# Gated feed-forward products over pairs of token tiles, a turned block of four heads' shifts, and window values laid out by tokens, in a fused sparse-attention and expert kernel

## What is computed

```
q, k, v   = 16 heads of width 16 from xn @ Wq, xn @ Wk, xn @ Wv
out_c     = softmax(q . compressed k of 32 blocks of 16 tokens) @ compressed v
top       = the 4 best blocks of each query
out_s     = softmax over the tokens of those 4 blocks @ v
out_l     = softmax over the last 33 tokens (a window) @ v
attention = (g0 out_c + g1 out_s + g2 out_l) @ Wo,   g = softmax(mean q @ Wg + bg)
mlp       = silu(xn @ Wg + bg) * (xn @ Wu + bu) @ Wd + bd,   1024 inner rows
experts   = product-key lookup: 4 heads, 8 of 1024 experts each, silu of their down product
out       = x + attention + mlp + experts
```

## Time and profile before

| | before |
|---|---|
| median of 3 runs | 1509.58 us (1504.55 to 1510.39) |
| the profiled execution's own time | 1507.87 us |
| its span | 1506.1 us |
| granted TensorE clock, mean | 0.979 of full |
| busy: PE, DVE, ACT, POOL | 1420.1, 1187.8, 928.4, 919.1 us |

### The profile page before, as it was taken

The page is one execution under the profiler, slowest core; times in us unless marked ns, Lnnn a source line. Parts: engine busy times, 40 slices in busy tenths (PEclk is TensorE's granted clock), DMA queues, the critical chain, the costliest instruction groups (busy, mean ns, idle before and its releaser), DMA issues. The chain is left out here.

```text
span 1506.1 us, 43877 instructions
## 1 busy us (share of the span) xinstructions
PE 1420.1 (94%) x14960; PEld 1044.1 (69%) x14960; DVE 1187.8 (79%) x4544; ACT 928.4 (62%) x1684; POOL 919.1 (61%) x845
## 2 busy tenths in 40 slices
PE   6899679999999999999999999999999999999978
PEld 4566447777777777777777777777777777777657
DVE  5444288888888888888888888898888888888812
ACT  3766336666666666666666666666666666666641
POOL 4655356666666666666666666666666666666620
PEclk8999879999999999999999999999999999999989
DMA  6556942221111122222111122212222222222027
GB/s 186 205 183 211 274 73 53 52 51 45 47 45 47 50 51 51 51 51 50 47 46 46 47 50 49 48 48 51 51 51 51 51 51 51 65 51 53 9 95 234
DMA packets 217147, 113.74 MB, mean 76 GB/s; under 512 B 128872, under 2 KB 211224, under 8 KB 217112
## 3 DMA queue, kind: packets, MB, share of 16 engines
q1 hardware_dynamic: 216304, 112.88, 27.3%
q10 hardware_dynamic: 808, 0.42, 0.2%
HBM read 73.08 MB, written 40.16 MB: 75 GB/s over the span
## 5 line engine op out<-in xcount | busy, mean ns | idle before, releaser
L1150 POOL TENSOR_TENSOR sumxy<-xy 128x1024 f32<-128x1024 f32 x128 | 240.7, 1901 | 0.0
L1393 DVE TENSOR_REDUCE bmax<-q_bank 128x32 f32<-128x512 f32 (+3 forms) x512 | 219.9, 481 | 16.5 <-PE q_bank L1633 15.4
L1240 ACT ACTIVATE pts<-k_bank 128x512 f32<-128x512 f32 (+2 forms) x384 | 177.4, 490 | 42.0 <-PE k_bank L1668 41.2
L1494 DVE SCALAR_TENSOR_TENSOR mw<-sumxy,c,ex 128x1024 f32<-128x1024 f32 x128 | 176.0, 1394 | 1.5 <-issue 0.8
L1633 PE MATMUL q_bank<-ko,qo 96*128 96x512 bf16 (+3 forms) x512 | 142.9, 306 | 24.6 <-DVE bmax L1393 22.6
L1116 POOL TENSOR_TENSOR pad<-pad 128x1 f32<-128x1 f32 x32 | 6.2, 193 | 256.4 <-DVE top L1412 256.4
L1615 PE MATMUL f_bank<-xt,wfu 128*128 128x128 f32 x1024 | 162.3, 281 | 0.0
L1174 POOL TENSOR_TENSOR cw<-cw,mw 128x1024 f32<-128x1024 f32 x64 | 150.8, 2356 | 6.6 <-ACT mw L1264 1.6
L1615 PE MATMUL f_bank<-xt,wfg 128*128 128x128 f32 x1024 | 150.3, 279 | 0.0
L1615 PEld LDWEIGHTS f_bank<-xt,wfu 128*128 128x128 f32 x1024 | 139.4, 191 | 11.5
L1264 ACT ACTIVATE mw<-mw,erec 128x1024 f32<-128x1024 f32 x128 | 145.7, 1139 | 0.0
(11 more groups left out here) (211 smaller groups left out, 3340.1 us busy)
## 6 DMA issues: line engine op xcount, KB each, us to landing
qo<-s_qs SPq DMA_DIRECT2D x192, 64.0 KB, 2.2
ko<-s_ks SPq DMA_DIRECT2D x186, 64.0 KB, 2.2
s_qs<-parts SPq DMA_DIRECT2D x8, 768.0 KB, 4.7
s_ks<-parts SPq DMA_DIRECT2D x8, 768.0 KB, 6.3
s_v<-vo SPq DMA_DIRECT2D x8, 544.0 KB, 3.0
vv<-s_v SPq DMA_DIRECT2D x32, 136.0 KB, 2.3
vw<-s_v SPq DMA_DIRECT2D x64, 68.0 KB, 2.5
xin<-in_L_attn_x_dram SPq DMA_DIRECT2D x8, 512.0 KB, 6.9
```

The lines of the kernel that those rows point to most:

```text
L1150: done("sum_done", g_.tensor_tensor(sumxy[:, h, :, :], xy[:, 0, h, 0:XK, None].broadcast_to([P, XK, KEYS]), xy[:, 1, h, None, :].broadcast ...
L1240: last = s.activation(pts[:, h, OFFS[j]:OFFS[j] + n], bank[:, 0:n], ACT.Exp)
L1393: last = v.tensor_reduce(bmax[:, i, h, 0:n], Q.bank(job)[:, o:o + n * BLK].rearrange("p (n j) -> p n j", j=BLK), AX.X, ALU.max)
L1494: done("mw_done", v.scalar_tensor_tensor(mw[:, h, :], sumxy[:, h, :, :].rearrange("p a b -> p (a b)"), c8[:, h, 7:8], ex[:, h % 2, :], ALU ...
```

## The change

1. **MLP up by pairs.** A unit moves both token tiles of its pair (`xp`, 256 tokens), but does half of the inner rows (4 `t.half` on). `up_rows` does one product of 256 columns in each call instead of two of 128. `mlp_down` adds 4 blocks of inner rows for each of the two tiles into Y, which now holds both tiles and is read once a pair; `xb` and `yo` follow.
2. **Shifts turned at once.** One `head_shifts` with 128 standing columns (4 heads by 32) fills one bank `a`. Head h's shift then stands in partitions 32h to 32h + 31, so `qo` and `ko` hold head h's shift or one-hot rows there and its q or k parts in the other three quarters; the places of shift rows are filled with zeros by DMA until the shift is there, and `queries` and `window` use 128 rows. ACT copies the four parts one by one: head 0 in `openings`, head 1 after `share(t, 2)`, heads 2 and 3 between the exponentials of head 0. Only the copy for head 3 releases the bank.
3. **Window values by tokens.** `local_values` has `pT` (32 columns) standing and `vw` (17 columns) moving and writes tokens by partitions, in two halves with the last `mlp_down` part split around the first; ACT's copy and PE's transposes of it go.
4. **Small ones.** DVE's `expert_sum` moves ahead of `key_marks`; some semaphores are merged.

The lists and loads (cut):

```
-            k_jobs = ["pcT", "co", "a0"]
+            k_jobs = ["pcT", "co", "a"]
             for h in range(HG):
-                k_jobs += [f"s{h}0", f"s{h}1", f"s{h}2"] + [f"a{h + 1}"] * (h < HG - 1) + [("pl0", "pl1", "vl", "tl")[h]]
-            k_jobs += ["vs", "ts"]
+                k_jobs += [f"s{h}0", f"s{h}1", f"s{h}2"] + [f"pl{h}"] * (h < 2)
+            k_jobs += ["vl", "vs", "ts"]
+            PARTS = ((0, 0), (2, 0)), ((0, 1), (0, 2)), ((1, 0), (1, 1))
+            N_NEAR, N_KEYS, N_QUERIES, N_LATE = (3, 4), 16, 20, (7, 8)
+            def part_rows(to, src, which, half):
+                for i, pair in enumerate(PARTS):
+                    lots = [(3, i, i + 1)] + [(i, h0, h1) for h0, h1 in ((0, i), (i + 1, HG)) if h0 < h1]
+                    for quad, h0, h1 in lots:
+                        for n in range(2):
+                            o = 32 * quad + D * n
+                            yield to[o:o + D, half, h0:h1, :], src[pair[n][which]][:, h0:h1, :]
                 def load_parts(b, g, half, keys=True):
+                    pairs = [(qo[32 * h:32 * h + 32, half, h, :], s_zero) for h in range(HG)]
+                    pairs += part_rows(qo, q, 0, half)
+                    if keys:
+                        pairs += part_rows(ko, k, 1, half)
```

ACT:

```
                         K.released(f"s{h}{j}", last)
-                    if h < HG - 1:
-                        head_shifts(t, h + 1)
+                        if h == 0 and j < 2:
+                            head_shifts(t, j + 2)
...
-                    if job == "g0":
-                        Y.wait_free(act, t, "y")
...
                 def head_shifts(t, h):
-                    K.wait_full(act, t, f"a{h}")
-                    K.released(f"a{h}", s.activation(qo[SP3:P, t.half, h, :], K.bank(f"a{h}")[SP3:P, :], ACT.Copy))
+                    if h == 0:
+                        K.wait_full(act, t, "a")
+                    rows = slice(32 * h, 32 * h + 32)
+                    copy = s.activation(qo[rows, t.half, h, :], K.bank("a")[rows, :], ACT.Copy)
+                    if h < HG - 1:
+                        done("aug_done", copy)
+                    else:
+                        K.released("a", copy)
...
                     share(t, 2)
+                    head_shifts(t, 1)
                     head(t, 0)
```

PE:

```
-                    o = P * (4 * j + k)
-                    dst = F.bank(f"{name}{j}")[:, k * P:k * P + P]
-                    for c in range(2):
-                        last = mm(dst, w_[:, c, o:o + P], xt[:, t.half, c, :], start=False, stop=(c == 1),
-                                  skip_group_check=True)
+                    f, c = divmod(k, 2)
+                    o = P * (4 * t.half + 2 * j + f)
+                    last = mm(F.bank(f"{name}{j}")[:, 2 * P * f:2 * P * f + 2 * P], w_[:, c, o:o + P], xp[:, c, :],
+                              start=False, stop=(c == 1), skip_group_check=True)
...
                 def keys_rows(t, h, part):
-                    if part == 0:
-                        K.wait_read(pe, t, f"a{h}")
+                    if part == 0 and h < HG - 1:
+                        need(pe, "aug_done", t, h + 1)
+                    elif part == 0:
+                        K.wait_read(pe, t, "a")
                     job = f"s{h}{part}"
                     K.wait_free(pe, t, job)
...
+                def local_values(t, r):
                     bank = K.bank("vl")
+                    rows = slice(64 * r, 64 * r + 64)
+                    for k in range(2):
+                        for g in range(T // 32):
+                            i, q = divmod(g, 4)
+                            o = VW * (HG * i + 2 * r + k)
+                            last = mm(bank[32 * q:32 * q + 32, o:o + VW], pT[rows, k, 32 * g:32 * g + 32],
+                                      vw[rows, t.half, g, VW * k:VW * k + VW], start=True, stop=True, skip_group_check=True)
...
                     for i in range(TT):
-                        last = mm(K.bank(f"a{h}")[SP3:P, P * i:P * i + P], shift_s[:, i, h, :], identb[:, :],
-                                  start=True, stop=True)
-                    K.filled(f"a{h}", last)
+                        last = mm(K.bank("a")[:, P * i:P * i + P], shift_s[:, i, :, :].rearrange("p h n -> p (h n)"),
+                                  identb[:, :], start=True, stop=True)
+                    K.filled("a", last)
...
-                            elif h == 2:
-                                local_ready(t)
-                            else:
-                                token_values(t, 1)
                             if h < 3:
                                 up_rows(t, "ugu"[h], (0, 1, 1)[h], part)
-                            else:
+                            elif part < 3:
                                 mlp_down(t, part)
-                            if (h, part) == (2, 3):
-                                local_values(t)
+                            if (h, part) == (3, 2):
+                                local_ready(t)
                             if n and part < 3:
                                 queries(n, h, part)
-                            if part == 2 and h < HG - 1:
-                                head_shifts(t, h + 1)
+                    local_values(t, 0)
+                    mlp_down(t, 3)
+                    local_values(t, 1)
                     selected_values(t)
```

More of the change, by code:

```diff
@@ L74, in count, with round @@
         return self.pair * (2 * per) + (self.offset * per + n)
+    def round(self):
+        return Round(self.pair, 0)
     def next(self, ahead=1):
         return Turn(self.pair, self.offset + ahead, step=self)
+class Round(Turn):
+    def count(self, per, n):
+        return self.pair * per + n
 class Chain:
@@ L1001, in hidden @@
             def hidden(j):
-                return hT[:, 4 * j:4 * j + 4, :].rearrange("p f t -> p (f t)")
+                return hT[:, 2 * j:2 * j + 2, :].rearrange("p f t -> p (f t)")
             def loaded_by(eng, lot, n, t):
+                n = n if isinstance(n, int) else n[t.half]
                 eng.wait_ge(lot[t.half], t.pair * (16 * n) + 16 * n * (t.offset // 2 + 1))
@@ L1039, in load_late @@
                           (gt[:, half, :, :].rearrange("p i n -> p (i n)"), row(s_gt, b)),
-                          (xb[:, half, :], row(tiles, b)[g]),
-                          *windows(b, g, half)], late_in[half], N_LATE)
+                          *both, *windows(b, g, half)], late_in[half], N_LATE[half])
                 def windows(b, g, half):
@@ L1183, in result_in @@
                     loaded_by(pool, late_in, N_LATE, t)
-                    done("xb_done", g_.tensor_tensor(xb[:, t.half, :], xb[:, t.half, :], bdb[:, :], ALU.add))
+                    done("xb_done", g_.tensor_tensor(xb[:, :, :], xb[:, :, :], bdb[:, None, :].broadcast_to([P, 2, C]), ALU.add))
                 def branches(t):
@@ L1312, in openings, with selected_values @@
                     tanh(t, "g0", hidden(0), "th_done")
-                def branch_values(t, k):
-                    job = ("vs", "vl")[k]
-                    K.wait_full(act, t, job)
-                    K.released(job, s.activation(oT[:, k, :], K.bank(job)[:, :], ACT.Copy))
+                def selected_values(t):
+                    K.wait_full(act, t, "vs")
+                    K.released("vs", s.activation(oT[:, :], K.bank("vs")[:, :], ACT.Copy))
                 def lead(n):
@@ L1593, in step @@
                     normalize(t, 0)
-                    result(t)
+                    if t.half:
+                        result(t)
                     cf.end()
@@ L1632, in queries @@
                         n = P * (i + 1)
-                        last = mm(bank[:, o:o + n], qo[0:SP3, t.half, h, P * i:P * i + P], ko[0:SP3, t.half, h, 0:n],
+                        last = mm(bank[:, o:o + n], qo[:, t.half, h, P * i:P * i + P], ko[:, t.half, h, 0:n],
                                   start=True, stop=(i > 0))
@@ L1693, in local_ready @@
                         K.wait_read(pe, t, f"pl{k}")
-                def local_values(t):
+                def local_values(t, r):
                     bank = K.bank("vl")
-                    for g in range(T // 32):
-                        for h in range(HG):
-                            rows, k = slice(64 * (h // 2), 64 * (h // 2) + 64), h % 2
-                            last = mm(bank[32 * h:32 * h + VW, 32 * g:32 * g + 32], vw[rows, t.half, g, VW * k:VW * k + VW],
-                                      pT[rows, k, 32 * g:32 * g + 32], start=True, stop=True, skip_group_check=True)
-                    K.filled("vl", last)
+                    rows = slice(64 * r, 64 * r + 64)
[5 more added lines that the diff above has]
+                                      vw[rows, t.half, g, VW * k:VW * k + VW], start=True, stop=True, skip_group_check=True)
+                    if r == 0:
+                        done("vl_half", last)
+                    else:
```

(6 more changed lines are left out.)

165 lines of the change are left out of this document (88 added, 77 removed).

## The result

The changed kernel takes 1597.01 us (median of 4, 1595.94 to 1602.08) against 1509.57 before: a ratio of 1.059, 95% interval 1.056 to 1.063. It is slower, as forecast, but by 87 us where I had 46, and 2 us above my range.

A forecast was written before the change was run, and what follows sets the result against it. PE bounds the step, except DVE from p01 to p21; +2.0 - 0.33 - 0.44 - 0.15 + 0.2 + 0.1 = +1.4 us a step, with the start 46 us on 1507.9: 1554 us, range 1503 to 1595.

The forecast's parts named there:

- The mechanism: PE waits ahead of s02 for ACT's last copy of bank a, 2.3 us; DVE then loses 2.0 us at p01.
- bank a holds nothing up: Rival at s02: PE is not held up and the savings win, 38.1 us a step, 1482 us; chance 0.14.
- both cancel: Rival: stall of 1.5 us against savings at their upper bounds, +0.4 us at most, 1508 to 1520 us; chance 0.12.
- The rival of cheap wide moving sides: Up products: half the weight loads take half the time, -1.1 us in place of -0.15, 1525 us; chance 0.08.
- The rival of SP's queue: Loads: at 0.5 to 0.6 us an issue, parts come 1.4 to 5 us late, 1600 to 1700 us; chance 0.08.
- the copy chain: ACT's copies with exponentials between, 2.57 us, ending at 734.71, so s02 starts 2.3 us late; +2.0 us a step.
- My upper bound: Stall of s02: 2.5 us if each of ACT's copies takes its full 0.59 us.
- the segment behind p21: Stretch at PE's pace, where savings count in full: head shifts -0.33 us, window value transposes -0.44 us.
- DVE's 2.25 us for candidates: DVE's wait for POOL's candidates would vanish with the earlier sum, worth nothing as PE sets the pace there.
- the window products: The 64 window value products, 1.39 us, stay and move behind s32 with sides exchanged; change taken as 0.
- the start: Start of the stage: 20 DMAs a queue ahead of the first queries instead of 6, 2 us, at most 6.4.
- the loads: 36 DMAs a unit instead of 12 on SP, landing 19.2 us after s32, cover nearly used up; +0.2 us a step.

The follow-up runs named there:

- experiment 1: Changed kernel with all four of ACT's shift copies ahead of the tanh of g0: 1532.42 us, ratio 1.015.
- experiment 2: Changed kernel with ACT's copies for heads 0 and 1 before the tanh of g0, 2 and 3 behind it, share 2 after the s00 exponential: 1504.13 us, ratio 0.996.
- experiment 9: Changed kernel with share 2 on ACT moved behind the exponentials of s01 and the last copy: 1551.11 us, ratio 1.028.
- experiment 11: Kernel before with only the shifts turned at once, including its 36 loads and zeros: 1616.93 us, ratio 1.072.
- experiment 5: Kernel before with only the paired up products, paired down product and paired result: 1506.45 us, ratio 0.998.
- experiment 3: Changed kernel with DVE's sum over the shares back behind the block maxima of head 2: 1611.63 us, ratio 1.067.
- experiment 6: Kernel before with paired products and window values by tokens and late, DVE's sum at its old place: 1521.44 us, ratio 1.009.
- experiment 7: Changed kernel with ACT's copies spread around the tanh and DVE's second up product ahead of unselected marks and best pairs: 1484.76 us, ratio 0.984.
- experiment 4: Kernel before with its 12 part loads split into 36 DMAs a unit and the setup store of zeros: 1528.97 us, ratio 1.012.

## Why the prediction was right and wrong

**The mechanism held.** PE idles ahead of s02 in each step, ended by ACT's last copy; experiments 1, 2, 9 and 11 take this wait away, shorten it or make it alone, and the time follows. DVE waits 2.59 us for p01 behind it. Rivals one and two (bank a holds nothing up; both cancel) fell with it. The rival of cheap wide moving sides fell as well: experiment 5 gains 0.2%. The rows have 0.22 to 0.24 us for an f32 record of 256 columns and 0.11 to 0.12 for 128. The rule of the Trainium skill ("TensorE: Matmul & The Clock Gate", "Back-to-back issue gap"), by which wide moving sides are cheap, is not borne out for them. The rival of SP's queue fell too: 36 issues took 0.48 us each (7.62 for 16), 17.5 us with gaps, a little more than I had; but a small DMA lands in 1.7 us, not 2.2, and that made up for it.

**The term that failed is the copy chain.** I wrote "A 512-column instruction takes 0.49 us from start to start" and gave that to the copies. They take 0.61, and the instructions ahead of them give up their overlap as well: from the first copy on I had 2.57 us, and it was 3.12 (778.25 to 781.37); from the tanh to the first copy I had 1.62 and it was 1.75 (776.50 to 778.25). That is 0.7 us more, of which PE, 0.1 later itself, feels 0.6: it idles 2.87 us ahead of s02 where I had 2.3. My upper bound, "2.5 us, if each copy takes its full 0.59", adds up (2.77 us of chain, s02 2.46 us late), but leaves the exponentials and share 2 their overlap, and so it was too low. The trace of before had it, with a lone copy of 32 rows whose neighbour starts 0.61 us later:

```profile
699.70 0.59 ACT L1308 ACTIVATE qo<-k_bank 32x512 bf16<-32x512 f32 x1 [1.11 <-PE k_bank L1754]
700.31 0.60 ACT L1248 ACTIVATE pT<-k_bank 128x512 f32<-128x512 f32 x1
```

I took the pitch from the tanh instead.

**Left out: the clock.** I had no term for a wait that slows PE afterwards. In 16 of 30 steps the front of head 1 runs at the lower level, and the step is 0.55 us longer: 8.8 us in all. The forecast had a wait of 2.3 us in it, and I did not ask what PE would do behind it. Part 1 of the same page of the Trainium skill says that the clock follows how busy the array has been of late; the trace agrees in so far as in the steady steps the clock falls only behind this wait (in the long step shown, 1.4 us after it has ended).

**Wrong: the segment behind p21.** I had -0.33 - 0.44 and some, about -0.8; from p21 to the product behind the window scores it was 11.40 for 11.45 us, so -0.05. The savings are there, and are given back: 0.57 us in the wait for the up product, and, net, some 0.13 in the products around the split down product. I had seen that the window values "move behind s32" and that DVE would be in slack, but not that these 1.35 us were what gave DVE time for the second up product. I had let DVE's 2.25 us for candidates vanish, rightly; that it buys something became true only through this wait (experiment 3). That these 1.35 us are the cause is supported by experiments 5 and 6, which change the form of the window products together with their place.

**Right in size:** the window products (0.66 us for each half from start to next start, 754.99 to 755.65, for 1.31 in one before), the start (2.3 us in the lead for 2, with PE waiting 4.25 us for the first k parts), and the loads (+0.2 forecast, no wait in the steady steps). The rest of the 7 us ahead of the first strike is not shown to be the change's.

The short step (776.51 to 817.71, by PE's block mask product behind s00) against a step of before (730.53 to 769.43), by PE's starts. "cw" is the turn of the expert weights, the first product behind the window scores:

| stretch | before | after | change | forecast |
|---|---|---|---|---|
| mask product to p01 | 2.69 | 5.47 | +2.78 | +2.1 |
| p01 to p21 | 8.97 | 8.85 | -0.12 | 0 |
| p21 to cw | 11.45 | 11.40 | -0.05 | -0.77 |
| cw to mask product | 15.79 | 15.48 | -0.31 | +0.05 |
| sum | 38.90 | 41.20 | +2.30 | +1.4 |

So 0.7 us more than forecast are the copies, and 0.7 the savings behind p21 that were given back; 0.5 came off elsewhere. Thirty steps of 2.30 make 69 us and the clock adds 8.8; of the remaining 3.6 of the 81.4, 2.7 lie in the first three steps behind the second strike (127.4 us, of which 1.1 for the clock, where three short steps are 123.6).

## What to carry to other kernels

When one long transfer replaces several short ones in a ring of banks, find the job that gets the bank next and add up the reader's program from the event that it hangs on, with the spacing that the rows show for that very form of instruction; an engine at 60% can still hold up one at 94% for 3 us. Changing the order of a few instructions in ACT's program costs nothing and was worth 93 us here. A block of work that moves may have been the time in which a neighbour got ready: ask of each thing that stood behind it what it will now wait for.

## What the chip showed that I had not expected

- ACT's copies of 32 rows by 512 columns into bf16 (0.59 us) do not overlap with the instructions ahead and behind: 0.61 us from start to start where 128-row ones have 0.49. Instructions of 112 rows by 128 columns do overlap (before, at 698.02 for 0.28, the next starting at 698.21), and so do those of 64 rows by 512 (before, three in 1.58 us). Whether it begins between 32 and 64 rows, and whether the bf16 output out of PSUM has a part in it, was not tried.
- After waits of 2.87 us PE's granted clock fell to its lower level for some 3 us in 16 steps of 30, with the wait already over (in 19 of 30 in experiment 3, and in 23 of 30 in experiment 11 with waits of 2.84 us); after waits of 1.74 us it never did. It is not tied to this place: in experiment 7 it fell once, 0.4 us behind a wait of 2.32 us for loads (267.11), and in experiment 4 behind one of 3.55 us (265.26). Why the falls come three or four in a row in the changed kernel is open, and so is from which wait on they begin.
- A DVE instruction of 0.41 us (marks of 128x512, f32 to bf16) takes 1.96 us beside POOL's sums. It starts at 750.46, 0.2 us behind the first of two sums (750.24), and ends at 752.42, 0.3 us after POOL has gone on to the second (752.10), as if it had waited for the first. With DVE's sum at its old place (experiment 3) the marks take 0.42 us again. That POOL is the cause is argued from these times only.
